# A graph and expert layer: sorted rows kept as two planes of 16-bit halves and turned by a DMA transpose

## The reference

```
xn = layernorm(x)
x = x + graph_attention(xn, edges; 8 heads of 32) + mixer(xn)[linear attention, MLP 256-768-256]
hn = layernorm(x)
probs = softmax(hn @ gate_w + gate_b)            # 8 experts
top2_vals, top2_idx = top_k(probs, 2)
for each expert e:                               # cw: the two top values at their experts, else 0
    x = x + cw[:, e] * (gelu(hn @ W1[e] + b1[e]) @ W2[e] + b2[e])
```

## Time and profile before

| | |
|---|---|
| median of three runs | 3769.97 us |
| profiled execution: span from first to last instruction | 3246.6 us |
| profiled execution's own time | not given by the page; the median lies 523.4 us above the span |
| PE busy | 2642.4 us, 81% |
| DVE busy | 2010.3 us, 62% |
| ACT busy | 1549.7 us, 48% |
| POOL busy | 2234.9 us, 69% |

### The profile page before, as it was taken

The page is one execution under the profiler, slowest core; times in us unless marked ns, Lnnn a source line. Parts: engine busy times, 40 slices in busy tenths (PEclk is TensorE's granted clock), DMA queues, the critical chain, the costliest instruction groups (busy, mean ns, idle before and its releaser), DMA issues.

```text
span 3246.6 us, 42100 instructions
## 1 busy us (share of the span) xinstructions
PE 2642.4 (81%) x11512; PEld 2052.3 (63%) x11512; DVE 2010.3 (62%) x5442; ACT 1549.7 (48%) x3382; POOL 2234.9 (69%) x2193
## 2 busy tenths in 40 slices
PE   8657767888888888888888887566359999999998
PEld 6546655666666665666656656344247888778887
DVE  7446557667777676777767766677654555445422
ACT  5325544544555554555455554334234545545444
POOL 0277777777777777777777777776476767676554
PEclk9879988999999999999999998777569999999999
DMA  9797766566666666666566665565766676766663
GB/s 276 242 295 211 199 178 169 162 173 177 164 172 180 172 172 170 174 179 171 163 180 172 173 169 153 160 181 136 253 198 146 151 160 148 162 142 131 131 110 62
DMA packets 397637, 561.15 MB, mean 173 GB/s; under 512 B 71912, under 2 KB 317950, under 8 KB 397225
## 3 DMA queue, kind: packets, MB, share of 16 engines
q0 software_dynamic: 123696, 298.61, 36.3%
q1 hardware_dynamic: 196473, 170.69, 18.1%
q10 hardware_dynamic: 77159, 88.50, 10.4%
HBM read 402.42 MB, written 169.68 MB: 176 GB/s over the span
## 4 chain that ended last, share of the span: by engine, by line
PE 65%; DMA 10%; ACT 8%; POOL 8%; issue 6%; DVE 2%; ACTq 0%; SPq 0%; POOLq 0%; DVEq 0%
PE bank L1314 21%; PE bank L2295 11%; PE bank L2308 10%; DMA rows<-table,srcix 9%; PE bank L1095 7%; POOL rows L1232 6%; PE bank L1084 5%; PE bank L1057 2%; PE bank L865 1%; PE bank L605 1%; PE bank L606 1%; ACT L1354 1%; PE bank L2284 1%; ACT xg L842 1%; PE bank L1296 1%
## 5 line engine op out<-in xcount | busy, mean ns | idle before, releaser
L1232 POOL DMA_INDIRECT rows<-table,srcix x1661 | 1600.3, 963 | 506.4 <-issue 354.2
L1314 PE MATMUL bank<-rows,onehot 128*128 128x272 f32 x3328 | 928.6, 426 | 57.4 <-ACT fout L1370 52.0
L1370 ACT ACTIVATE fout<-bank 128x272 f32<-128x272 f32 x1659 | 638.6, 397 | 574.7 <-PE bank L1314 525.3
L1314 PEld LDWEIGHTS bank<-rows,onehot 128*128 128x128 f32 x3328 | 666.5, 208 | 244.3 <-ACT fout L1370 78.7
L1463 DVE TENSOR_TENSOR rows<-rows,bank 128x1024 f32<-128x1024 f32 x416 | 484.0, 1213 | 173.2 <-ACT rows L1359 172.8
L2386 POOL DMA_INDIRECT out<-x_y,x_dest x203 | 325.0, 1601 | 233.2 <-DMA out<-x_y,x_dest 173.4
L2295 PE MATMUL bank<-x_int,x_w1c 128*128 128x256 f32 (+1 forms) x1696 | 379.7, 378 | 25.5 <-issue 22.2
L2308 PE MATMUL bank<-e_w,x_ht 128*128 x1624 | 370.5, 381 | 9.5 <-issue 7.0
L2295 PEld LDWEIGHTS bank<-x_int,x_w1c 128*128 128x128 f32 x1696 | 316.4, 194 | 77.4 <-issue 35.6
L2334 ACT ACTIVATE x_ht<-bank,x_b1c 128x256 f32<-128x256 f32 (+1 forms) x424 | 173.1, 462 | 394.4 <-PE bank L2295 392.9
L2308 PEld LDWEIGHTS bank<-e_w,x_ht 128*128 128x128 f32 x1624 | 300.2, 190 | 51.3 <-issue 14.8
(11 more groups left out here) (405 smaller groups left out, 3246.3 us busy)
## 6 DMA issues: line engine op xcount, KB each, us to landing
frag<-fout ACTq DMA_DIRECT2D x104, 544.0 KB
rows<-table,srcix POOLq DMA_INDIRECT x1661
x_in<-sorted_d SPq DMA_DIRECT2D x97, 260.0 KB, 3.5
x_b2c<-in_L_ffn_b SPq DMA_DIRECT2D x106, 128.0 KB, 3.5
frag<-in_x ACTq DMA_DIRECT2D x1, 13416.0 KB
table<-hr SPq DMA_DIRECT2D x24, 544.0 KB, 4.0
xs<-in_x SPq DMA_DIRECT2D x24, 512.0 KB, 6.0
xg<-in_x SPq DMA_DIRECT2D x24, 512.0 KB, 6.4
```

What stands on the lines that cost most here:

```text
L1232: p.indirect_dma_start(out=B.rows[b][:, j, :], out_offset=None, in_=B.table[:, :], in_offset=bass.IndirectOffsetOnAxis(ap=B.srcix[:, col:c ...
L1314: pe.matmul(B.banks[2 + c % 3][:, 0:ROW], B.onehot[k % 2][:, j, :], B.rows[k % NR][:, j, :], start=True, stop=True).then_inc(S.sum, 1)
L1370: a.activation(B.fout[k % 2][:, j, :], B.banks[2 + c % 3][:, 0:ROW], ACT.Copy).then_inc(S.ev, 1)
```

## The change

A row of sorted_d is now 272 four-byte words (1088 bytes). It is laid out as two planes: the low 16-bit halves of the 256 features, then 16 halves of padding that hold the tail's four words, then the high halves. Seen as 16-bit values, sorted_d is a matrix with two rows per node row. VectorE writes this form from e_hn into a new buffer e_hs (three of them) with one copy per super-tile of four node tiles (split); e_hn has one buffer in place of three. The sends read e_hs. SyncE loads a tile with dma_start_transpose: 512 rows x 256 half-words come back as features on partitions and, per node, low and high half side by side, which is the float again, in x_int (three buffers in place of two). TensorE's turns, bank 4 and ScalarE's copy are gone. The tail, 16 bytes a row, comes by a second load. NOUT is 5 in place of 6, and the buffer of a fetch is free when fc1 of its last tile is done in place of its turn.

```diff
-SENT = D + 4
+PLANE = D + 16
+SENT, TAIL, TAILS = PLANE, D // 2, 4
...
-NOUT = 6
+NOUT = 5
...
-        self.sorted_d = dram("sorted_d", [ZERO_ROWS + ET, SENT])
+        self.sorted_d = nc.dram_tensor("sorted_d", [ZERO_ROWS + ET, SENT], I32, kind="Internal").ap()
+        self.sorted_f = self.sorted_d.bitcast(F32)
+        self.planes_d = self.sorted_d.bitcast(U16).rearrange("n (h f) -> (n h) f", h=2)
...
-                             in_=B.e_hn[r % NH][:, i, :], in_offset=None).then_inc(S.e_g[r % NH], 16)
+                             in_=B.e_hs[r % NH][:, i, :], in_offset=None).then_inc(S.e_g[r % NH], 16)
...
         a.wait_ge(S.e_mom, r + 1)
-        if r >= NH:
-            a.wait_ge(S.e_g[r % NH], sent_to(r - NH))
+        if r:
+            a.wait_ge(S.e_tp, 2 * 2 * r)
+            a.wait_ge(S.e_split, 2 * r)
...
+    def split(r):
+        if r >= NH:
+            v.wait_ge(S.e_g[r % NH], sent_to(r - NH))
+        for k in ROUNDS[r]:
+            s, m = SUPERS[k]
+            at = slice(s - R_FIRST[r], s - R_FIRST[r] + m)
+            v.wait_ge(S.e_hn, s + m)
+            planes = B.e_hs[r % NH][:, at, :].bitcast(U16).rearrange("p t (h f) -> p t h f", h=2)[:, :, :, 0:D]
+            v.tensor_copy(planes, B.e_hn[:, at, :].bitcast(U16).rearrange("p t (f h) -> p t h f", h=2)).then_inc(S.e_split, 1)
+            yield
+        yield from idle(SPLITS - len(ROUNDS[r]))
...
+        yield from idle(waits)
+        yield from split(r)
...
         if j >= NI:
-            sp.wait_ge(S.x_tp, j - NI + 1)
+            sp.wait_ge(S.x_f1, 2 * (j - NI + 1))
             sp.wait_ge(S.x_aim, j - NI + 1)
-        sp.dma_start(B.gin[u][:, 0:SUBS[j], :], B.sorted_d[bass.ds(at, SUBS[j] * P), :].rearrange("(t p) d -> p t d", p=P)).then_inc(S.x_in[u], 16)
+        n = SUBS[j] * P
+        sp.dma_start_transpose(B.gt[u][:, :, 0:n].bitcast(U16), B.planes_d[bass.ds(at * 2, 2 * n), 0:D]).then_inc(S.x_in[u], 16)
+        sp.dma_start(B.x_tail[u][:, 0:SUBS[j], :],
+                     B.sorted_f[bass.ds(at, n), TAIL:TAIL + TAILS].rearrange("(t p) d -> p t d", p=P)).then_inc(S.x_tail[u], 16)
...
-    def start(j):
-        u = j % NI
-        pe.wait_ge(S.x_in[u], 16 * (j // NI + 1))
-        pe.wait_ge(S.x_gt, j)
-        for k in range(KD):
-            for i in range(SUBS[j]):
-                t = pe.transpose(bk[BANK_IN][:, k * ET + i * P:k * ET + (i + 1) * P], B.gin[u][:, i, k * P:(k + 1) * P], B.ident[:, :])
-        t.then_inc(S.x_tp, 1)
...
     def first(j):
-        u, n = j % 2, SUBS[j] * P
-        pe.wait_ge(S.x_gt, j + 1)
+        u, x, n = j % 2, B.gt[j % NI], SUBS[j] * P
+        pe.wait_ge(S.x_in[j % NI], 16 * (j // NI + 1))
...
     def start(j):
-        a.wait_ge(S.x_tp, j + 1)
         if j >= 2:
             a.wait_ge(S.x_f1, 2 * (j - 1))
-        n = SUBS[j] * P
-        a.activation(B.gt[j % 2][:, :, 0:n], B.banks[BANK_IN][:, :].rearrange("p (k n) -> p k n", k=KD)[:, :, 0:n], ACT.Copy).then_inc(S.x_gt, 1)
```

More of the change, by code:

```diff
@@ L1703 @@
 SPREAD = 3
+SPLITS = 6
 FIRST_ROUNDS = 2
@@ L1851, in steps @@
                 for i in range(m):
-                    t = pe.transpose(bk[kk][:, i * P:(i + 1) * P], B.e_hn[r % NH][:, o + i, kk * P:(kk + 1) * P], B.ident[:, :])
+                    t = pe.transpose(bk[kk][:, i * P:(i + 1) * P], B.e_hn[:, o + i, kk * P:(kk + 1) * P], B.ident[:, :])
                 t.then_inc(S.e_tp, 1)
@@ L1977, in sums @@
                                op1=ALU.mult).then_inc(S.e_mom, 1)
+    def split(r):
[9 more added lines that the diff above has]
+        yield from idle(SPLITS - len(ROUNDS[r]))
     def steps(r):
-        n, s0, hn = R_TILES[r], R_FIRST[r], B.e_hn[r % NH]
-        if r == 1:
-            yield from idle(FRONT)
-        else:
+        n, s0, hs = R_TILES[r], R_FIRST[r], B.e_hs[r % NH]
+        waits = FRONT - SPLITS
+        if r != 1:
             yield from sums(r)
-            waits = FRONT - MOMENTS - MOMENT_STEPS
+            waits -= MOMENTS + MOMENT_STEPS
             if r == 0:
@@ L1989, in steps @@
                 waits -= MOMENTS + MOMENT_STEPS
-            yield from idle(waits)
+        yield from idle(waits)
+        yield from split(r)
         L, Pr, K, both, pos = (t[:, 0:n, :] for t in (B.lg, B.pr, B.key, B.both, B.pos))
@@ L2294, in first @@
             for k in range(KD):
-                t = pe.matmul(out, B.w1c[u][:, k, m * P:(m + 1) * P], B.gt[u][:, k, 0:n], start=(k == 0), stop=(k == KD - 1))
+                t = pe.matmul(out, B.w1c[u][:, k, m * P:(m + 1) * P], x[:, k, 0:n], start=(k == 0), stop=(k == KD - 1))
             if m % 2:
@@ L2310, in second @@
         t.then_inc(S.x_f2, 1)
-    return tile_order(first=first, start=start, second=second)
+    return tile_order(first=first, second=second)
 def experts_scalar(a, S, B):
     def start(j):
-        a.wait_ge(S.x_tp, j + 1)
         if j >= 2:
             a.wait_ge(S.x_f1, 2 * (j - 1))
-        n = SUBS[j] * P
-        a.activation(B.gt[j % 2][:, :, 0:n], B.banks[BANK_IN][:, :].rearrange("p (k n) -> p k n", k=KD)[:, :, 0:n], ACT.Copy).then_inc(S.x_gt, 1)
         a.wait_ge(S.planned, planned_by(j))
@@ L2343, in start @@
         u, o, n = j % NI, j % (NOUT + 1), SUBS[j]
-        tail = lambda col: B.gin[u][:, 0:n, D + col]
+        tail = lambda col: B.x_tail[u][:, 0:n, col]
         dest, scale = B.dest[o][:, 0:n], B.scale[o][:, 0:n]
@@ L2348, in start @@
             v.wait_ge(S.x_st, 2 * (j - NOUT))
-        v.wait_ge(S.x_in[u], 16 * (j // NI + 1))
+        v.wait_ge(S.x_tail[u], 16 * (j // NI + 1))
         v.wait_ge(S.planned, planned_by(j))
```

35 lines of the change are left out of this document (20 added, 15 removed).

## The result

On the same chip the kernel after took 3741.56 us (median of 4 runs, 3736.97 to 3742.74) and the kernel before 3769.68 us (4 runs, 3763.11 to 3783.53). The ratio is 0.9896, 95% interval 0.9861 to 0.9931: 1.0% faster, some 39 us by the ratio. The two medians by themselves lie 28 us apart, a ratio of 0.9925. Why the two ratios differ so much here is not known; in the later comparisons they differ by 0.0014 at most. Two later comparisons of the same two kernels gave 0.9904 (0.9875 to 0.9933) and 0.991 (0.9875 to 0.9944). The mean of the three ratios is 0.9903, 36 us. The forecast was 3778 us, no change.

What follows compares the result with a forecast made beforehand. The prediction took GpSimd's chain of adds and their landings as the bound; +4.5 - 1.5 + 0 + 5 + 0 = +8 on the median of 3769.97 gave 3778 us, no change, range 3732 to 3850.

Steps and rivals of the forecast that it cites:

- I take 0 for the turns: Expert stage: removing 43.7 us of turns from TensorE gains nothing, as GpSimd's chain of adds sets the end.
- the lag of 20 us: Mid expert stage: results lay 20.3 and 21.2 us before GpSimd issued their adds, so GpSimd was taken as the bound.
- The rival with the chance of 0.11: Expert stage: TensorE sets the pace, so the turns' time is won, -39 us, 3731 us; chance 0.11.
- The first rounds (+4.5): First round: two splits on VectorE ahead of the logits delay the first send by 2 x 2.27 = 4.5 us.
- The first tile (-1.5): Start of the experts: no turn or copy before fc1, and fewer early waits for results, -1.5 us for both.
- Splits against GpSimd: 25 splits on VectorE stretch GpSimd instructions beside them by about 0.5 us each or nothing; 5 us taken.
- 25 us more as a rival: Splits hold GpSimd up for their whole length: 25 x 1 us more, 3798 us; chance 0.09.
- The quarter: GpSimd beside a split: stretch of about a quarter of the split's length, read from another kind of instruction.
- Neither rival about them: GpSimd's adds land sooner (3750 us, chance 0.11) or later (3834 us at 1 us per wait, chance 0.20).
- The landing times that I had named as a sign: Adds' landing time moving from 4.4 to 4.7 us by more than 0.3 us would show the prediction wrong.
- The transposed load: SyncE's load of a tile by transpose: same bytes as the plain load, 0 us taken, bounds -28 to +132 us.
- The rival by which a load would take longer than a tile: SyncE's queue: transposed loads set the tile's period, +194 us at 10 us each, 3970 us; chance 0.05.

Runs made afterwards that it cites:

- the second profile of before: The kernel before, unchanged, profiled once more: span 3736.1 us at a time of 3737.38 us.
- before with one add: The kernel before with only the first of the two adds of each full tile: ratio 0.9935 to before.
- before with five results: The kernel before with NOUT = 5 in place of 6, nothing else: ratio 1.0012 to before.
- with the weights sooner: The kernel before with ScalarE's copy of the next tile's first weights put ahead of this tile's gelus: ratio 0.9993 to before.
- before with the turns alone: The kernel before with TensorE's turns kept and ScalarE's copies of the turned rows left out: ratio 1.0 to before.

## Why the prediction was wrong

**The step that failed: "I take 0 for the turns".** It follows from "GpSimd has hardly ever waited for the experts" and the lag of 20 us, and these were read rightly, but from an execution that isn't like the timed ones. In the timed executions GpSimd's chain of adds is not what sets the end: leaving out the turns and their copies gave 44 us in place of 0, doing the turns twice cost 84, halving the adds gave 24 and not 184. The sign that this could be so stood in my own sum: 3246.6 us of span under 3770 us of time. A remainder of 523 us, a sixth of the span, can't be let stand: either it lies outside the span, or the execution is another one. In the profile after the remainder is 1.2 us, and in the second profile of before 1.3.

**The rival with the chance of 0.11 had the right number, in part by luck.** "TensorE is the bound after all" priced the change at 43.7 less 4.5, 39 us, and the ratios say 39, 36 and 34. What spoke for it was the page's chain; what I held against it came from one execution. But it counts every microsecond of the turns as won, and by themselves they were worth 22 us in before and about 16 in after; it gives the copies nothing, which is what they gave alone, and turns and copies together gave 44. And with half of the adds left out of both kernels it would have after some 40 us below before, where the two are alike (0.9951 and 0.9935). So the runs show that the gain comes from leaving out turns and copies, and that GpSimd's chain isn't the bound; that TensorE's busy time by itself is, they don't show.

The two chains lie near each other. In the first profile GpSimd's was the longer by some 3% (its 846 us less 11.5 of waits for results are 834, and TensorE was busy for 806), and in ordinary executions the stage is 66 us, 8%, longer, with GpSimd busy no longer than there.

**The terms of the sum.** TensorE's slot: 0.43 us, as sized; 44.0 us less busy in the stage. The first rounds (+4.5): from the first logits to the first send it is 10.30 us after (2765.62 to 2775.92) and 10.29 in the second profile of before, so only what stands ahead of the logits counts. The splits there take 2.35 us for two, the lower end of my bounds and half of the value I took. I had chosen it by element count; the copy handles 2048 half-words in the time in which VectorE does 1024 whole ones. The first tile (-1.5): from its load's issue to fc1 it is 22.8, 19.5 and 21.3 us in the three profiles of after, and 25.8 in the second of before; before with one add and before with five results had 23.5 and 32.0, so a term of 1.5 can't be told from the stops.

**Splits against GpSimd.** I took 5 us for it and named 25 us more as a rival. The rival's mechanism is what the trace shows: the send at 2955.92 takes 2.33 us, until just behind the end of the two splits at 2958.12, where its neighbours take 0.98. Beside another pair of splits the sends at 3173.09 and 3175.04 take 1.65 and 1.55 us. By group means, the 196 sends take 1037 ns for 998, 7.5 us in all, and the adds 1596 for 1590, 1.3 us. Together 9 us of GpSimd's time in this profile, more than the 5 of the sum; in the second profile of after the sends of the stage have a mean of 1007 ns, so even this is near the noise. No run shows what it cost the whole.

The Trainium skill (SBUF — State Buffer, Who interferes with whom) says that a copy in a mode that uses both ports blocks GpSimd for its whole length. By that rule, this trace agrees: 2.33 us against 0.98, though the trace doesn't name the copy's mode. The quarter that I had taken from another kind of instruction was the wrong row.

**Landings.** Neither rival about them was it. The waits for landings did get longer in total (81.0 to 124.1 us), but they do so without the turns on a plain load too (152.0, 138.6). There are more of them, 40 in place of 24, and the mean of one is 3.1 us in place of 3.4. A wait for a landing that appears where a wait for a result was is not a slower landing. The landing times that I had named as a sign aren't given in the profiles of ordinary executions.

**The transposed load** cost nothing that can be told from the noise, as I took. TensorE never waited for it in the stage of the profile after; SyncE waited for fc1 for 187.3 us (for the earlier trace rows, from 2861 us on):

```profile
SPq L2282 <- PE bank L2312: 187.3, 70, 7.2
```

The rival by which a load would take longer than a tile is out: tiles follow at 6.91 us.

## What to carry to other kernels

Before reading who waits for whom, lay the profiled execution's span beside the timed runs: where they differ by hundreds of microseconds, the profile may be of an execution of another kind, and a bound that is won by a few per cent in it can be lost in the timed ones. Price each candidate bound by the stage (in the first profile TensorE was busy for 806 us of it, and GpSimd busy or tied up with its own chain for 834), and where two lie that close give both real chances. Kernels with one engine's work doubled or halved say more than a lag of 20 us or a list of waits: here both pointed at GpSimd, and halving its work gave 24 us once and nothing twice.

## What the runs showed that I had not expected

The same program has executions nearly without stops and with many: 3246.6 us in one profile of before, and 3736.1 in the other, with all of its timed runs between 3690 and 3802 us. In the ordinary ones several engines stand still for 3 to 8 us at a time, with nothing in the trace that they wait for. I can't say what these stops are; no run took them away.

TensorE stood still more after than before. In the three profiles of after the stage less TensorE's busy time is 110.5, 109.6 and 103.7 us; in before it is 88.1, 82.3 with five results and 72.6 with the weights sooner. It isn't simply that less work leaves more standing: before without turns and copies has 84.9 us with a busy time as short as after's, and before with the turns alone has 108.1 with a busy time as long as before's. What decides it was not found.

Work of two engines along one hand-over need not add up: 0 us for the copies, 22 for the turns, 44 for both.
